# Twelve experts in flight, and the down product of two tiles on the two row halves of the array

## The reference

```
h = tok(x)                                    # 448 x 512
h = h + bitlinear_mlp(layernorm(h))           # weights rounded to -1, 0, 1
xn = layernorm(h)
probs = softmax(xn @ router_w.T)              # 32 experts
rw, sel = top_k(probs, 8);  rw = rw / sum(rw)
for e in range(32):                           # w_gate, w_up: 512 x 192, w_down: 192 x 512
    acc += (silu(xn @ w_gate[e]) * (xn @ w_up[e])) @ w_down[e] * weight(token, e)
out = h + acc
```

## Time and profile before

| | |
|---|---|
| median of 3 runs (358.29 to 361.75) | 358.31 us |
| the profiled execution's own time | 358.37 us |
| its span, first to last instruction | 356.4 us |
| mean granted TensorE clock | 0.913 |
| TensorE busy | 82% of the span |
| VectorE, ScalarE, GpSimd busy | 42%, 36%, 41% |
| bytes moved | 85.50 MB, mean 240 GB/s |

### The profile page before, as it was taken

The page is one execution under the profiler, slowest core; times in us unless marked ns, Lnnn a source line. Parts: engine busy times, 40 slices in busy tenths (PEclk is TensorE's granted clock), DMA queues, the critical chain, the costliest instruction groups (busy, mean ns, idle before and its releaser), DMA issues.

```text
span 356.4 us, 3752 instructions
## 1 busy us (share of the span) xinstructions
PE 292.6 (82%) x1107; PEld 155.9 (44%) x1107; DVE 150.1 (42%) x447; ACT 127.9 (36%) x208; POOL 146.7 (41%) x137
## 2 busy tenths in 40 slices
PE   6799764186877928999999999999999999949840
PEld 1344322144544704555555555555555555523210
DVE  3438789545657860243343323323233233222320
ACT  3245818993895321132222223223222232221000
POOL 4404445662552130334444454453544544233170
PEclk9999996578998955999999999999999999987995
DMA  7599950049208842599999999999999999997722
GB/s 295 194 359 419 370 181 3 0 134 329 70 0 246 257 143 70 177 313 310 276 296 300 313 323 311 326 305 321 311 309 313 292 323 304 279 300 165 196 92 74
DMA packets 23540, 85.50 MB, mean 240 GB/s; under 512 B 3569, under 2 KB 3697, under 8 KB 22753
## 3 DMA queue, kind: packets, MB, share of 16 engines
q1 hardware_dynamic: 15152, 64.54, 53.8%
q0 software_dynamic: 7968, 20.26, 23.6%
q10 hardware_dynamic: 402, 0.48, 0.4%
HBM read 72.34 MB, written 12.92 MB: 239 GB/s over the span
## 4 chain that ended last, share of the span: by engine, by line
PE 55%; DVE 18%; issue 9%; DMA 6%; ACT 6%; POOL 3%; POOLq 0%; DVEq 0%; ACTq 0%
PE ps L1032 24%; PE ps L1061 14%; PE ps L1052 4%; DMA sum<-w_t,add_idx 4%; DVE stats L1166 3%; PE ps L1017 2%; PE ps L910 2%; PE ps L1081 2%; PE ps L860 2%; PE ps L936 2%; ACT w_t L678 2%; DVE raw L1267 1%; POOL root_out L509 1%; DVE big L1261 1%; DVE amax L1314 1%
## 5 line engine op out<-in xcount | busy, mean ns | idle before, releaser
L581 POOL DMA_INDIRECT big<-token_rows,idx x36 | 35.9, 997 | 104.9 <-DVE idx L1407 81.9
L592 POOL DMA_INDIRECT sum<-w_t,add_idx x32 | 50.9, 1589 | 17.0 <-issue 8.8
L1419 DVE SCALAR_TENSOR_TENSOR w_t<-ps,big,w_t 128x192 f32<-128x192 f32 x32 | 13.4, 418 | 103.3 <-issue 89.5
L1032 PE MATMUL ps<-ring,w_t 128*128 128x384 f32 x128 | 48.1, 521 | 0.2 <-ACT w_t L789 0.2
L794 ACT ACTIVATE w_t<-ps 128x192 f32<-128x192 f32 x34 | 11.3, 331 | 96.0 <-PE ps L1032 90.1
L509 POOL TENSOR_TENSOR root_out<-root_in,minus_half 112x1 f32<-112x1 f32 x20 | 12.8, 640 | 59.1 <-DVE root_in L1179 59.0
L910 PE MATMUL ps<-w_t,q_t 128*112 128x512 bf16 (+1 forms) x96 | 26.0, 429 | 9.9 <-DVE h L1217 5.9
L860 PE MATMUL ps<-raw,turned 128*112 128x512 f32 x64 | 30.2, 621 | 4.3 <-issue 2.3
L800 ACT ACTIVATE w_t<-ps 128x512 f32<-128x512 f32 x32 | 19.1, 597 | 37.2 <-PE ps L1061 36.0
L1032 PEld LDWEIGHTS ps<-ring,w_t 128*128 128x128 f32 x128 | 24.1, 198 | 17.4 <-issue 4.8
L1052 PE MATMUL ps<-ident,big 128*128 128x128 f32 x136 | 22.9, 293 | 9.4 <-DMA big<-token_rows,idx 9.4
(11 more groups left out here) (178 smaller groups left out, 426.2 us busy)
## 6 DMA issues: line engine op xcount, KB each, us to landing
ring<-in_ffn_gate_up SPq DMA_DIRECT2D x20, 768.0 KB
ring<-in_ffn_w_down SPq DMA_DIRECT2D x20, 384.0 KB, 5.3
big<-in_ffn_gate_up SPq DMA_DIRECT2D x10, 768.0 KB
raw<-in_ffn_gate_up SPq DMA_DIRECT2D x10, 768.0 KB
big<-in_ffn_w_down SPq DMA_DIRECT2D x10, 384.0 KB
raw<-in_ffn_w_down SPq DMA_DIRECT2D x10, 384.0 KB, 6.4
big<-in_mlp_w_in SPq DMA_DIRECT2D x2, 1536.0 KB, 10.5
big<-in_mlp_w_in SPq DMA_DIRECT2D x2, 1280.0 KB, 13.8
```

What stands on the lines that cost most here:

```text
L581: nc.gpsimd.indirect_dma_start(got[:, s, :], None, rows_dram[:, :], bass.IndirectOffsetOnAxis(ap=idx[:, s:s + 1], axis=0)).then_inc(ld_got ...
L592: nc.gpsimd.indirect_dma_start(acc_dram[m.two][:, :], bass.IndirectOffsetOnAxis(ap=add_idx[:, m.four:m.four + 1], axis=0), y[:, m.four, :] ...
L1032: last = nc.tensor.matmul(dst, x_t[:, m.two, c, :], wg[:, :, c, :], start=c == 0, stop=c == 3)
```

## The change

- **Slots.** `R = 12` instead of 8. Several small buffers of the first part now share one piece of memory (`scrap`), and the slots lie over what is free earlier. Experts 1 to 3 load as soon as the first sign pieces are done, 10 and 11 after the first gathered tile has been turned. List n of the quads waits for tile 20 + n. SyncE no longer waits for `bc_done` before the first weight load.
- **Down product.** The 192 rows of a down matrix are split 128 and 64 instead of 96 and 96. The 64 go to partitions 0 to 63 for an even slot and 64 to 127 for an odd one. Two tiles are done together: both 128-row products, then both 64-row products, which stand in different row halves of the array and write different banks. `down_two(t-2)` runs in the even steps alone; `transpose_h` of an odd tile moves to the step after it. `turn_back`, `y_out` and `scatter` follow in twos.
- **Idle products.** `keep_busy(8)` ahead of the first place rows and `keep_busy(14)` behind them: products of 112 rows and 448 columns in bf16 whose result nobody reads.
- **Quads.** `gate_up_lists(a)` goes ahead of `transpose_x(b)`; both spreads stand last, as eight products. The gather of the second quad no longer waits for tile 31. The weight of a list's tokens comes from one product and one multiply instead of four register loads and copies. The second sum is read back in two halves.

```diff
-R = 8
+R = 12
...
+        def rest_rows(n):
+            return slice(n % 2 * IB, (n % 2 + 1) * IB)
         def down_of(n):
-            return slots[n][0:IH, WG:WCOLS].rearrange("p (c d) -> p c d", c=2)
+            return slots[n][:, WG:WG + D]
+        def down_rest_of(n):
+            return slots[n][rest_rows(n), WG + D:WCOLS]
...
-            sp.wait_ge(bc_done, 4)
...
             def load_down(e, n):
-                sp.dma_start(slots[n][0:IH, WG:WCOLS], we_down_v[e, :, :]).then_inc(ld_dn[n], 16)
+                sp.dma_start(down_of(n), we_down[e, 0:P, :]).then_inc(ld_dn[n], 16)
+                sp.dma_start(down_rest_of(n), we_down[e, P:IE, :]).then_inc(ld_dn[n], 16)
...
             load_expert(0)
-            sp.wait_ge(wd_ready, 1)
-            load_expert(1)
+            for t, signs in ((1, 3), (2, 5), (3, 8)):
+                sp.wait_ge(wt_ready, signs)
+                load_expert(t)
...
+            sp.wait_ge(z_done, NG)
+            sp.wait_ge(xt_done, 1)
+            load_expert(10)
+            load_expert(11)
...
# GpSimd, for t in range(NE)
-                if t:
-                    scatter(Tile(t - 1))
+                if t % 2 and t >= 3:
+                    scatter(Tile(t - 3))
+                    scatter(Tile(t - 2))
...
# GpSimd, gather
-                if isinstance(m, Quad):
+                if isinstance(m, Quad) and not isinstance(m.k, int):
                     pool.wait_ge(hid_ready, m.upto(-2))
...
# ScalarE, for t in range(NE)
+                if t % 2 and t >= 3:
+                    y_out(Tile(t - 3))
+                    y_out(Tile(t - 2))
                 act.wait_ge(gu_done, t + 1)
                 silu(m)
                 if t + 1 < NE:
                     x_turned(Tile(t + 1))
-                if t:
-                    y_out(Tile(t - 1))
...
# TensorE
+            def down_two(t):
+                for m in (Tile(t), Tile(t + 1)):
+                    pe.wait_ge(ht_ready, m.upto())
+                    pe.wait_ge(ld_dn[m.slot], 2 * m.loaded())
+                    wait(pe, y_ready, m.upto(-2))
+                    nc.tensor.matmul(bank(4 + m.two), h_t[:, m.two, 0, :], down_of(m.slot), start=True, stop=False)
+                for m in (Tile(t), Tile(t + 1)):
+                    rows_ = rest_rows(m.slot)
+                    nc.tensor.matmul(bank(4 + m.two), h_t[rows_, m.two, 1, :], down_rest_of(m.slot), start=False, stop=True
+                                     ).then_inc(y_done, 1)
...
+            def keep_busy(count):
+                for _ in range(count):
+                    nc.tensor.matmul(bank(3)[:, 0:TOK], ident16[0:G, :], before[:, 0, :], start=True, stop=True)
+            keep_busy(8)
             pe.wait_ge(place_ready, 1)
...
+            keep_busy(14)
             transpose_x(Tile(0))
...
                 gate_up(Tile(t))
+                if t and t % 2 == 0:
+                    transpose_h(Tile(t - 1))
                 if t + 1 < NE:
                     transpose_x(Tile(t + 1))
-                if t:
-                    down(Tile(t - 1))
-                transpose_h(Tile(t))
-            down(Tile(NE - 1))
+                if t % 2 == 0:
+                    if t:
+                        down_two(t - 2)
+                    transpose_h(Tile(t))
+            transpose_h(Tile(NE - 1))
+            down_two(NE - 2)
...
                 transpose_x(a)
+                gate_up_lists(a)
                 transpose_x(b)
-                gate_up_lists(a)
                 gate_up_lists(b)
                 transpose_h(a)
+                place_lists(Quad(k + 1, 0))
                 down_lists(a)
                 transpose_h(b)
-                place_lists(Quad(k + 1, 0))
-                spread_lists(a)
                 place_lists(Quad(k + 1, 1))
                 down_lists(b)
-                spread_lists(b)
+                spread_lists((a, b))
...
# VectorE, for t in range(NE)
+                if t and t % 2 == 0:
+                    turn_back(Tile(t - 1))
                 dve.wait_ge(ld_got[m.four], m.gathered())
                 weigh(m, got[:, m.four, D + t:D + t + 1])
                 if t + 3 < NE:
                     find(Tile(t + 3))
...
-                turn_back(m)
+                if t % 2 == 0:
+                    turn_back(m)
                 keep(m)
+            turn_back(Tile(NE - 1))
```

More of the change, by code:

```diff
@@ L49, in __init__ @@
     def __init__(self, t):
-        self.t, self.slot, self.two, self.four = t, t % R, t % 2, t % 4
+        self.t, self.slot, self.two, self.four, self.eight = t, t % R, t % 2, t % 4, t % 8
     def upto(self, d=0):
@@ L109, in program, with early @@
         w_in_raw = big[:, :].rearrange("p (b d) -> p b d", b=22)
-        vec_row = big[0:1, 0:4 * D]
+        scrap = sb("scrap", [128, 12 * D], F32)
         at = [0]
-        def late(cols, dt=F32):
+        def early(cols):
             at[0] += cols
[L116 to L123, removed]
+            assert at[0] <= 12 * D
+            return scrap[:, at[0] - cols:at[0]]
+        h_work = early(2 * D)[0:G, :].rearrange("p (s d) -> p s d", s=2)
+        q1_t = early(DC * TOK // 2).bitcast(BF16).rearrange("p (c t) -> p c t", c=DC)
+        bias_bc, g2_bc, b2_bc, gin_bc = [early(D)[0:G, :] for _ in range(4)]
+        gdn_bc = early(I1)[0:G, :]
+        junk = early(3 * D // 2).bitcast(BF16)
+        at[0] = 0
+        rows = early(NG * ROW)[0:G, :].rearrange("p (g r) -> p g r", g=NG)
+        got = early(4 * ROW).rearrange("p (s r) -> p s r", s=4)
+        mask_pm = early(TOK)[0:NE, :]
+        y_list = early(2 * D).rearrange("p (s d) -> p s d", s=2)
+        swg = big[0:G, 22 * D - 2 * I1:22 * D].rearrange("p (s i) -> p s i", s=2)
         w_t = sb("w_t", [128, DC * 2 * I1], BF16)
@@ L151, in program @@
         swi = raw_flat[0:G, 0:2 * I1].rearrange("p (s i) -> p s i", s=2)
-        slots = [ring[:, n, :] for n in range(4)] + [
-            big[:, 11 * D + 2 * I1:11 * D + 2 * I1 + WCOLS], raw[:, 0, :], raw[:, 1, :], big[:, 11 * D:11 * D + WCOLS]]
-        turned = sb("turned", [128, IC * TOK // 2], F32)
+        slots = [ring[:, 0, :], big[:, 0:WCOLS], big[:, WCOLS:2 * WCOLS], big[:, 2 * WCOLS:3 * WCOLS], ring[:, 1, :], ring[:, 2, :],
+                 ring[:, 3, :], raw[:, 0, :], raw[:, 1, :], big[:, 3 * WCOLS:4 * WCOLS], last[:, 0:WCOLS],
+                 last[:, WCOLS:2 * WCOLS]]
         patch_t = [turned[:, n * KC * G:(n + 1) * KC * G].rearrange("p (b t) -> p b t", b=KC) for n in range(2)]
@@ L159, in program @@
         h = sb("h", [G, NG, D], F32)
[L160 to L169, removed]
+        part = [h, scrap[0:G, 0:NG * D].rearrange("p (g d) -> p g d", g=NG)]
         gb_c = sb("gb_c", [128, 2 * KC], F32)
@@ L283, in program @@
         added = [sem(f"added{n}") for n in range(2)]
-        ld_part = sem("ld_part")
+        ld_part = [sem(f"ld_part{n}") for n in range(3)]
         dve_chain = sem("dve_chain")
@@ L812, in _ @@
                     x_turned(Tile(t + 1))
-                if t:
-                    y_out(Tile(t - 1))
+            y_out(Tile(NE - 2))
             y_out(Tile(NE - 1))
@@ L1045, in gate_up_lists @@
                         if c == 3:
-                            last.then_inc(gu_done, 1)
+                            last.then_inc(gu_done, R - NLIST + 1 if m.i == 1 and u == 3 else 1)
             def transpose_x(m):
@@ L1409, in keep @@
             def keep(m):
-                s = m.four
-                if m.t >= 4:
-                    dve.wait_ge(added[m.two], m.added() - 32)
-                nc.vector.tensor_copy(add_idx[:, s:s + 1], idx[:, s:s + 1]).then_inc(add_ready, 1)
+                if m.t >= 8:
+                    dve.wait_ge(added[m.two], m.added() - 64)
+                nc.vector.tensor_copy(add_idx[:, m.eight:m.eight + 1], idx[:, m.four:m.four + 1]).then_inc(add_ready, 1)
             def weigh(m, gate):
@@ L1503, in _ @@
                     turn_back(m)
-                for i in range(2):
-                    find(Quad(k + 1, i))
+                    find(Quad(k + 1, m.i))
                 dve.wait_ge(total_ready, NG)
```

165 lines of the change are left out of this document (91 added, 74 removed).

## The result

The changed kernel takes 365.15 us (median of 4 runs, 364.11 to 366.45), the kernel before 359.19 beside it: a ratio of 1.0156, 95% interval 1.0085 to 1.0227. By the medians it is 6.0 us slower, by the ratio 5.6. The profiled execution took 364.18 us with a span of 362.4. Each ratio is the one on record with its interval and can lie up to 0.4% from the quotient of the medians. One run of the study, of 411.87 us at a mean clock of 0.733 in experiment 6, is slow and left out.

The account below looks back on a forecast made before the run. TensorE was taken to bound the loop, with DMA nearly used up. Tile 31 beginning 8.1 us later (first stretch's 2.9 gain included), less 6.2 at the end, gave +1.9 on 358.37: 360.3, say 360 us; range 352 to 370.

Parts of the forecast that it names:

- Rival 1: Down's 64-row halves do not run side by side: 367 us for three passes (chance 0.12), 374 for four (0.08).
- Rival 3: In the loop, gathers come late behind two scatters: 9 us more, 369 us; chance 0.10.
- tile 1's start: End of the first stretch: tile 1 begins at 140.4 us, against 143.31 before.
- the loop: Tile 1 to tile 31: a pair takes 11.70 us against 10.96, 0.74 slower; tile 31 begins at 317.2.
- the end: From the end of tile 31's gate and up to the last add: 27.7 us against 33.9, 6.2 gained.
- Idle products: First stretch: they keep the clock up for tile 0, 2.9 us gained; bounds -1 and 3.1.
- Odd step: Loop step without down products: its place row waits for VectorE's index; 4.93 us, 1.49 of it idle.
- Even step: Loop step with both tiles' down products: 6.77 us, with 0.86 for paired 64-row halves and 0.2 for shape changes.
- Twelve slots: Weight slots in the loop: four more cover nothing, as TensorE waits for no weights with eight.
- TensorE's spreads take the place of the adds: Last stretch: eight spreads standing last take 7 us, end at 27.1 and set the last add at 27.7.
- column strips: Quads' weight loads: four float32 products ran fully side by side; the same taken for row halves, 0.86 us saved per pair.
- Rival 2: Odd step does not idle: pair 10.2 us, loop 22 us shorter but limited by DMA; 343 us; chance 0.08.

Follow-up runs that it names:

- experiment 6: experiment 2 with both 64-row parts of the down products in the same row half: 358.98 us, ratio 0.9938 to the kernel before.
- experiment 3: Changed kernel with 26 instead of 14 idle products ahead of tile 0: 363.94 us, ratio 1.0106 to the kernel before.
- experiment 4: Kernel before with only idle products added, 8 ahead of the place rows and 26 ahead of tile 0: 357.89 us, ratio 0.9953.
- experiment 1: Changed kernel with VectorE's search put ahead of the weighing in the odd steps: 350.78 us, ratio 0.9764 to the kernel before.
- Experiment 10: Kernel before with one edit, the second quad's gather no longer waiting for tile 31 to be weighed: 354.31 us, ratio 0.9805.
- experiment 7: Changed kernel with weight loads held to eight ahead instead of twelve, slots left in place: 368.7 us, ratio 1.0283 to the kernel before.
- experiment 5: Changed kernel with the 64-row parts of both tiles in the same row half: 378.4 us, ratio 1.0528 to the kernel before.
- experiment 2: experiment 1 plus, in odd steps, the next tile's x turned ahead of gate and up and copied ahead of silu: 345.93 us, ratio 0.9627.
- experiment 8: experiment 2 with weight loads held to eight ahead instead of twelve: 348.44 us, ratio 0.9707 to the kernel before.

## Why the prediction was right or wrong

The time, 365.15 us, lies in the range of 352 to 370, 5 us above the predicted 360. Slower was forecast, by 1.9 us, which I had called no different from no change. The forecast's own interval, 354.7 to 361.9, was missed. Only rivals 1 and 3 carried the range up to 370, and both are false, so it is in part luck that the time lies in it. Of the 4.9 us over 360.3, tile 1's start has 2.9, the loop 1.6, the end -0.3 and what lies around the last add and the span -0.3; the last 1.0 is that the median lies above the profiled execution.

- **Idle products, predicted -2.9, measured 0: this step failed.** I reckoned that the fourteen would take "5.5 us at half clock and 2.8 at full" and set only the delay against them, not the gap: at full clock they cover 2.8 of the 4.81 us. The uncovered 2.40 us are followed by a clock of 0.50, and tile 0 took 5.49 us. Experiments 3 and 4 give the term back (-2.8 and -3.0) by making the products last. The bounds of -1 and 3.1 held the result. The half clock that I had reckoned with stood in one profiled execution, and there fourteen were enough (experiment 3). The mechanism, a higher clock for tile 0, was right; the cover of the gap was not.
- **Odd step, predicted 4.93, measured 4.92.** Tile 0 of the kernel before had shown it. That the order of search and weighing causes it is shown by experiment 1.
- **Even step, predicted 6.77, measured 6.91: a term mis-sized.** From the timeline: gate and up 2.68, turned blocks 0.22, x 0.48, 128-row products 1.82 (1.72 predicted; a pass of 512 columns takes 0.43 with 128 rows as with the 96 of before), 64-row parts with their changes 1.06 (0.86 + 0.2 predicted), hidden values 0.37 (0.32), place row 0.28. The last 128-row pass and both 64-row passes take 0.52 to 0.53 instead of 0.43: going over to 64 rows and back costs 0.3 in a pair, where I had 0.2. With 15 pairs the step's 0.14 is 2.1 us.
- **The loop, predicted +11.0 from tile 1 to 31** (317.2 - 140.4 against 165.8), **measured +12.6.** The even step gave 2.1 more; what comes on top of the pairs, tables and the like, was 0.9 and not 1.3.
- **The end, predicted 27.7 from the end of tile 31's gate and up, measured 27.44.** The sum was right, its reason in part: I gave the gain to several moves at once. Experiment 10 shows that the freed gather alone gives 5.0 of the 6.45 us, by way of the scatters behind it; experiment 7 that the early lists carry 4.0, by way of the same scatters. These overlap, since 5.0 + 4.0 is more than 6.45. Twelve slots, which I had put at nothing, thus count, though only here. That TensorE's spreads take the place of the adds was half right: they end at 351.08, just ahead of VectorE's last add, but VectorE's adds begin on GpSimd's, at 349.30, and without the spreads would have ended no earlier.
- **Rival 1, halves not side by side: false**, and by experiment 5 it would have cost 13.3 us (13.8 predicted). The column strips were the right row to reason from the earlier trace rows. The records of two float32 products, two each, started 0.00 and 0.01 us apart, in two passes and not in three or four. The changes of shape cost the 0.3 us a pair named above; what the engine does in that time no run shows.
- **Rival 2, no idle in the odd step: false for this kernel, and its price nearly right by luck.** Experiment 2 makes it true and takes 345.9, against 343. But 343 leaned on a bound of transfers that doesn't hold: a DMA share of 1.06 was no bound, and experiments 6 and 8 show room for both the faster pair and eight slots. Without it my own terms give 360.3 - 22 = 338; tile 1's late start (3.5), the pair of 10.47 instead of 10.2 (with the tables 3.0) and the longer end (1.2) make up the rest.
- **Rival 3, late gathers: false.** No gather wait stands in the changed kernel's loop; TensorE waits there for VectorE's index alone, 16 times, 20.2 us in all.

## What to carry to other kernels

A change that takes work off the bounding engine also takes the cover from every wait that stood behind that work. List, for each step that gets shorter, what the next one waits for and where that stands in its own engine's queue; here moving one call each on VectorE, TensorE and ScalarE turned +6.0 us into -14.0. Of a wait that is added or removed, count what is queued behind it: one gather's wait was worth 5 us through a scatter that had nothing to do with it. Filler that is to hold the clock has to be reckoned at full clock too, not only at the lower one: fourteen products took 5.17 us at 0.50 and covered the gap, and 2.82 at 1.00 and left 2.40 us of it, after which the clock fell to 0.50. What 26 would cost in an execution in which they start at 0.50 no run shows; at 5.17 / 14 each they would take 9.6 us, an estimate, and delay tile 0.

## What the runs showed of the hardware

- A DMA share of 1.05 to 1.06 stood beside 286 GB/s with TensorE waiting for VectorE, beside 315 before, and beside 313 in experiment 2. The share didn't tell whether transfers bound the loop.
- After the idle products TensorE was idle for 2.40 us at a clock that read 1.00, and the clock fell to 0.50 within the next two stages, while TensorE was busy again. After an idle time of 0.26 us (experiment 3) it stayed at 1.00.
- Two 64-row products on different row halves, each of 512 columns in float32, take 1.06 us together, and 1.91 in the same half. Going from 128-row to 64-row products and back costs about 0.3 us: three passes of 0.52 to 0.53 instead of 0.43.
